# Constants on ScalarE's queue, x in pieces, the last two rows stored by hardware queues, output halves summed on TensorE

## The reference

```
e   = x + par[0]*par[1] * (diag[:, None] * x) @ W     # users: first 2048 rows, items: the rest,
                                                      # each with its own par, diag, W
h   = adj @ (adj.T @ e)
out = layernorm(h) * gamma + beta + x
x   = layernorm(x + out)                              # end of layer 0

T1  = adj @ x;  T2 = 2*adj @ T1 - x;  T3 = 2*adj @ T2 - T1
out = x @ w[0] + T1 @ w[1] + T2 @ w[2] + T3 @ w[3] + bias
x   = layernorm(x + out)                              # end of layer 1, the result
```

## Time and profile before

| | us |
|---|---|
| median of three executions | 1214.84 |
| lowest and highest of them | 1209.78, 1215.15 |
| the profiled execution's own time | 1212.09 |
| its span, first to last instruction | 1210.2 |

### The profile page before, as it was taken

How to read it: one execution, slowest core, us unless ns; L and a number is a source line. 1 busy time by engine, 2 the same in 40 slices (tenths; PEclk the granted TensorE clock), 3 DMA queues, 4 the chain that set the end, 5 groups by cost and what they waited for, 6 DMA issues and landing times.

```text
span 1210.2 us, 13868 instructions
## 1 busy us (share of the span) xinstructions
PE 1109.8 (92%) x5004; PEld 479.3 (40%) x5004; DVE 922.2 (76%) x960; ACT 332.1 (27%) x594; POOL 257.6 (21%) x420
## 2 busy tenths in 40 slices
PE   4999999999999997899889999999999999598794
PEld 3454445444444453444233333344344443122231
DVE  2698798999899898697777766665666667588783
ACT  1456456456466465300000000000100000011010
POOL 0476655464363453100000000000000000011111
PEclk9999999999999999899999999999999999798898
DMA  7999999999999987899999999999999999999991
GB/s 227 300 289 298 282 299 315 289 296 279 299 275 282 296 233 167 186 313 286 266 347 347 336 313 293 318 292 255 261 336 319 336 304 330 348 306 342 353 352 30
DMA packets 372730, 350.82 MB, mean 290 GB/s; under 512 B 11612, under 2 KB 371332, under 8 KB 372692
## 3 DMA queue, kind: packets, MB, share of 16 engines
q1 hardware_dynamic: 259092, 237.35, 70.5%
q10 hardware_dynamic: 110880, 110.11, 31.8%
q0 software_dynamic: 2720, 2.86, 0.9%
HBM read 348.97 MB, written 1.31 MB: 289 GB/s over the span
## 4 chain that ended last, share of the span: by engine, by line
PE 55%; SPq 12%; DVE 12%; ACT 10%; ACTq 5%; issue 4%; POOL 1%; DMA 1%; DVEq 0%; POOLq 0%
PE bank L1174 31%; ACT terms L774 9%; SPq L337 7%; ACTq L279 5%; SPq L326 4%; DVE turned L496 4%; PE bank L1225 4%; PE bank L1187 3%; PE bank L1044 2%; PE bank L1004 2%; PE bank L1032 2%; PE bank L1056 2%; PE bank L1016 2%; DVE shared L516 2%; PE bank L1203 1%
## 5 line engine op out<-in xcount | busy, mean ns | idle before, releaser
L1174 PE MATMUL bank<-turned,terms 128*128 128x512 f32 x680 | 301.4, 596 | 4.5 <-DVE turned L496 3.1
L386 POOL COPY raw<-raw 32x512 f32<-32x512 f32 x320 | 194.8, 609 | 243.6 <-DVE raw L533 205.1
L516 DVE STREAM_TRANSPOSE shared<-shared 32x512 f32<-32x512 f32 x320 | 224.0, 700 | 4.1
L1004 PE MATMUL bank<-shared 128*64 128x256 f32 x1600 | 206.1, 385 | 6.5 <-DMA shared<-in_adj 6.4
L496 DVE STREAM_TRANSPOSE turned<-raw 128x2048 f32<-128x2048 f32 x72 | 165.1, 2301 | 58.9 <-PE bank L1174 50.0
L496 DVE STREAM_TRANSPOSE turned<-shared 128x2048 f32<-128x2048 f32 x68 | 156.0, 2302 | 60.3 <-PE bank L1174 46.0
L774 ACT COPY terms<-terms 32x512 f32<-32x512 f32 x320 | 197.1, 616 | 5.1 <-DVE terms L526 0.9
L1174 PEld LDWEIGHTS bank<-turned,terms 128*128 128x128 f32 x680 | 126.6, 190 | 170.3 <-issue 164.0
L431 POOL DMA_DIRECT2D out<-scratch x40 | 21.7, 549 | 681.1 <-DVE scratch L724 681.0
L1004 PEld LDWEIGHTS bank<-shared 128*64 128x64 f32 x1600 | 111.6, 136 | 88.4 <-issue 33.1
L765 ACT COPY scratch<-bank 128x512 f32<-128x512 f32 x80 | 46.6, 585 | 131.2 <-PE bank L1016 130.9
(11 more groups left out here) (144 smaller groups left out, 1059.7 us busy)
## 6 DMA issues: line engine op xcount, KB each, us to landing
shared<-in_adj SPq DMA_DIRECT2D x100, 1024.0 KB, 10.7
raw<-in_adj SPq DMA_DIRECT2D x106, 512.0 KB, 10.6
raw<-in_adj ACTq DMA_DIRECT2D x106, 512.0 KB, 12.3
shared<-in_adj SPq DMA_DIRECT2D x104, 512.0 KB, 10.6
shared<-in_adj ACTq DMA_DIRECT2D x104, 512.0 KB, 12.1
raw<-in_adj SPq DMA_DIRECT2D x80, 256.0 KB, 7.6
xq<-in_x POOLq DMA_DIRECT2D x40, 32.0 KB, 6.2
out<-scratch POOLq DMA_DIRECT2D x40, 32.0 KB, 5.2
```

Source lines behind the costliest of these rows:

```text
L386: last = nc.gpsimd.tensor_copy(moved[Q32 * c:Q32 * (c + 1), :, :, Q32 * q:Q32 * (q + 1)], beside[Q32 * q:Q32 * (q + 1), :, c, :, :])
L516: last = nc.vector.transpose(low_turned[Q32 * c:Q32 * (c + 1), :, :, Q32 * q:Q32 * (q + 1)], low[Q32 * q:Q32 * (q + 1), :, :, Q32 * c:Q32 ...
L1004: last = nc.tensor.matmul(t_bank[H * odd:H * (odd + 1), 0:PW], e[:, s * SB + b, :], panels[slot][:, s * SB + b, :], start=(k == 0 and b < ...
L1174: last = nc.tensor.matmul(sum_bank[parity][:, :], terms[:, c * GB + i, columns], turned[place][:, i * BANK:(i + 1) * BANK], start=(first a ...
```

## The change

Three parts. First, the head: `W` and `par` are issued by ACT instead of SP; `diag` gets a semaphore of its own, `diag_loaded`, which PE's turning of `diag` now waits for; DVE copies `diag` before it waits for the six other constants; `x` comes by five transfers with a semaphore each, which DVE waits for piece by piece. Second, the end: POOL stores only the first eight rows of the output; SP stores row n = 8 and half of row n = 9, ACT the other half, and SP waits for both rows to land. Third, in `turn_output` each of the four transposes becomes a matmul with `both` as the moving operand, so that the two halves are added in it and 64 columns come out of each; in `finish` the copy and the addition become one copy of 128 x 256.

```diff
         consts_loaded = sem("consts_loaded")
-        x_loaded = sem("x_loaded")
+        diag_loaded = sem("diag_loaded")
+        x_loaded = [sem(f"x_loaded{k}") for k in range(NS)]
...
+        last_stored = sem("last_stored")
...
+        def store(queue, n, q, stored):
+
+            queue.dma_start(quarter(out, ROWS3[n], q),
+                            by_chunk(scratch[Q32 * q:Q32 * (q + 1), 2 + n % 2, 0:GB * H], H)).then_inc(stored, DMA)
+
...
         def _(sp):
-            sp.dma_start(diag_rows[0:UB, :], diag_u.rearrange("(b p) -> b p", p=P)).then_inc(consts_loaded, DMA)
-            sp.dma_start(diag_rows[UB:NB, :], diag_i.rearrange("(b p) -> b p", p=P)).then_inc(consts_loaded, DMA)
-            sp.dma_start(e[:, :, :], x.rearrange("(b p) f -> p b f", p=P)).then_inc(x_loaded, DMA)
-            sp.wait_ge(w_cleared, 1)
-            for k, a in enumerate((W_u, W_i)):
-                for half in range(2):
-                    rows_of = slice(H * half, H * (half + 1))
-                    sp.dma_start(w_pair[rows_of, k, rows_of], a).then_inc(consts_loaded, DMA)
-            for k, a in enumerate((par_u, par_i)):
-                sp.dma_start(par[:, 2 * k:2 * k + 2], a.rearrange("(o n) -> o n", o=1).to_broadcast([P, 2]))\
-                    .then_inc(consts_loaded, DMA)
-
+            sp.dma_start(diag_rows[0:UB, :], diag_u.rearrange("(b p) -> b p", p=P)).then_inc(diag_loaded, DMA)
+            sp.dma_start(diag_rows[UB:NB, :], diag_i.rearrange("(b p) -> b p", p=P)).then_inc(diag_loaded, DMA)
+            x_rows = x.rearrange("(b p) f -> p b f", p=P)
+            for k, s in enumerate(SEGS):
+                b = slice(s * SB, (s + 1) * SB)
+                sp.dma_start(e[:, b, :], x_rows[:, b, :]).then_inc(x_loaded[k], DMA)
...
+            for n in (NG - 2, NG - 1):
+                sp.wait_ge(out_made, n + 1)
+                for q in range(NQ if n == NG - 2 else NQ // 2):
+                    store(sp, n, q, last_stored)
+            sp.wait_ge(last_stored, DMA * NQ * 2)
...
         def _(pool):
-            for n, g in enumerate(ROWS3):
+            for n in range(NG - 2):
                 pool.wait_ge(out_made, n + 1)
                 for q in range(NQ):
-                    pool.dma_start(quarter(out, g, q), by_chunk(scratch[Q32 * q:Q32 * (q + 1), 2 + n % 2, 0:GB * H], H))\
-                        .then_inc(out_stored[n % 2], DMA)
+                    store(pool, n, q, out_stored[n % 2])
             for k in range(2):
-                pool.wait_ge(out_stored[k], DMA * NQ * (NG // 2))
+                pool.wait_ge(out_stored[k], DMA * NQ * (NG // 2 - 1))
...
         def _(dve):
-            dve.wait_ge(consts_loaded, DMA * 8)
+            dve.wait_ge(diag_turned, 1)
+            chain(nc.vector.tensor_copy(diag[:, :], t_bank[:, 0:NB]))
+            dve.wait_ge(consts_loaded, DMA * 6)
...
-            dve.wait_ge(diag_turned, 1)
-            chain(nc.vector.tensor_copy(diag[:, :], t_bank[:, 0:NB]))
-            dve.wait_ge(x_loaded, DMA)
-            for s in SEGS:
+            for k, s in enumerate(SEGS):
                 b = slice(s * SB, (s + 1) * SB)
+                dve.wait_ge(x_loaded[k], DMA)
                 nc.vector.tensor_tensor(xq[:, b, :], e[:, b, :], wide(diag[:, b], SB), ALU.mult).then_inc(x_scaled, 1)
...
-                halves = by_chunk(out_bank[n % 2][:, :], PH)
-                chain(nc.vector.tensor_copy(y, halves[:, :, 0:H]))
-                nc.vector.tensor_tensor(y, halves[:, :, H:PH], y, ALU.add).then_inc(out_taken, 1)
+                nc.vector.tensor_copy(y, by_chunk(out_bank[n % 2][:, 0:GB * H], H)).then_inc(out_taken, 1)
...
         def _(act):
+
+            act.wait_ge(w_cleared, 1)
+            for k, a in enumerate((W_u, W_i)):
+                for half in range(2):
+                    rows_of = slice(H * half, H * (half + 1))
+                    act.dma_start(w_pair[rows_of, k, rows_of], a).then_inc(consts_loaded, DMA)
+            for k, a in enumerate((par_u, par_i)):
+                act.dma_start(par[:, 2 * k:2 * k + 2], a.rearrange("(o n) -> o n", o=1).to_broadcast([P, 2]))\
+                    .then_inc(consts_loaded, DMA)
...
             root(2 * NS + NG - 1, GB)
+            act.wait_ge(out_made, NG)
+            for q in range(NQ // 2, NQ):
+                store(act, NG - 1, q, last_stored)
...
-            pe.wait_ge(consts_loaded, DMA * 8)
+            pe.wait_ge(diag_loaded, DMA * 2)
...
                 for c in range(GB):
-                    last = nc.tensor.transpose(out_bank[i % 2][:, c * P:(c + 1) * P], o_turned[:, c * P:(c + 1) * P],
-                                               ident[:, :])
+                    last = nc.tensor.matmul(out_bank[i % 2][:, c * H:(c + 1) * H], o_turned[:, c * P:(c + 1) * P],
+                                            both[:, :], start=True, stop=True)
```

## The result

| | before | after |
|---|---|---|
| median, us | 1214.63 | 1202.53 |
| lowest and highest of five | 1209.78, 1215.15 | 1199.89, 1205.22 |
| the profiled execution's own time | 1212.09 | 1205.22 |
| its span | 1210.2 | 1203.1 |

The medians differ by 12.1 us. The ratio of the times is 0.9912, with a 95% interval of 0.9886 to 0.9938, which is 10.7 us faster (7.5 to 13.8), against 12.7 predicted.

A forecast was written before the change was run, and what follows sets the result against it. Transfers of `adj` were taken to bound the kernel up to about 170 us, then a cycle of its engines, with 11.36 us without arithmetic at the end. 4.4 + 8.3 + 0 = 12.7 us saved gave 1200 us, range 1194.5 to 1207.

The forecast's parts named there:

- Term 4.4: Head: the first panel of `adj` starts earlier once the constants leave SP's queue; 4.4 us saved, bounds nothing and 5.5.
- the 5.5 of the whole gap: Head: transfer engines nearly idle between `x` and the first panel, 14.7 - 9.2 = 5.5 us, the term's upper bound.
- the 1.1 us taken off for `W`, `par` and the ramp: Head: allowances against the gap, 0.5 us for carrying `W` and `par`, 0.6 for the hand-over to the panel.
- the near end of the two that the prediction kept: Head: constants issued by ACT land near 9 to 10 us, or near 15 if they block behind `x`.
- The sign that failed: Layer 0's first panels: copies of `t` of panels 2, 7 and 20 each some 4.4 us earlier.
- Term 8.3: End: after DVE's last instruction 3.0 us in place of 11.36, POOL's DRAIN lying under sweep 3; 8.3 us saved.
- its upper bound of 9.0: End: with the fastest issues and a landing of 1.8 us, the moved stores save 9.0 us.
- Term 0: Output turning and summing: PE's added work and DVE's saved work cancel in the last row, others are covered; 0 us.
- A: Head: rival, the panel doesn't start earlier, the first term falls to about 0.5 us; 1204 us, chance 0.14.
- B: End: rival, POOL's DRAIN of 7 us stays at the end of the program; 1207 us, chance 0.10.
- C: Head: rival, ACT's constants are starved behind `x` and the panels, landing at 32.6; slower, 1219 us, chance 0.04.

The follow-up runs named there:

- the stores alone: Only the change's stores (rows 8 and 9 by SP and ACT, POOL eight rows) on the kernel before: 1204.71 us, ratio 0.9931.
- the repeat: The whole change once more, same kernel, for a second profile, timed against the kernel before: 1200.48 us, ratio 0.9904.
- the head alone: Only the change's edits of SP, DVE, ACT and PE at the start, on the kernel before: 1209.12 us, ratio 0.9961.
- the cut of the tiles on the kernel before: The kernel before with layer 0's tile loads cut in eight transfers in place of four, nothing else: 1208.77 us, ratio 0.9965.
- turning: Only the summing by the turning matmul, on the kernel before: 1213.3 us, ratio 1.0002.
- row 8 kept: The kernel before with only row 9 stored by SP and ACT, POOL keeping row 8: 1203.94 us, ratio 0.9926.
- `x` in one transfer: The whole change, but x in one transfer as before, in place of five: 1200.38 us, ratio 0.99.

## Why the prediction was right, point by point

**The head.** Term 4.4, measured alone 4.7 (3.3 to 6.3 by the interval). The mechanism is shown by the gap, which goes with the new head and comes back with the constants on SP's queue, and by the lead of the transfers at 8 MB: 4.7 to 5.2 us with the constants on ACT, 0.8 with them on SP. That lead lies between the 4.4 of the term and the 5.5 of the whole gap; of the 1.1 us taken off for `W`, `par` and the ramp, 0.3 to 0.8 are seen. What the prediction did not have is that part of the lead is lost again in the panels behind it. So the gain in time is known less well than the lead: what the whole has beyond the stores alone (0.9912/0.9931, and 0.9904/0.9931 in the repeat) is 2.3 and 3.3 us, each to some 3 us. These and 4.7 agree with 4.4 within their intervals; that the kernel with the head alone came so near to it is in part luck. The waits told rightly that the transfers lead up to about panel 7, as the cut of the tiles on the kernel before shows. The constants issued by ACT were landed at 9.2, by the near end of the two that the prediction kept.

The rule of the Trainium skill that spoke against this term ("DMA: Bandwidth & Descriptors", "Issuing engines are not separate DMA queues") grants a second issuer only its sequencer's time. The traces decide otherwise here: with the six small transfers in SP's queue the engines' share is 0.05 and 0.16 from 10.5 to 13.5 us, with another issuer for them 1.08.

**The sign that failed.** "The copy of `t` of panels 2, 7 and 20 each some 4.4 us earlier" held for the second profile of the same kernel (5.1, 3.8, 3.8) and not for the first (1.7, 0, 0). The prediction had said what it would mean for the copies to be earlier at panel 2 but not at 7: that the engines' cycle led there. That reading is wrong. From panel 2 to 7 a panel takes (170.85 - 55.32)/5 = 23.1 us in the first profile, the engines' cycle is 22.1 by the cut tiles, and the product waits 10.2 us for transfers: they led there too. Two things failed. One is the assumption that one profiled execution gives this number to within a few tenths: for one kernel it moved by 3.9 us at panel 7 (170.85 and 167.00), with times of 1205.22 and 1200.0. The other is that panel 7 moves by as much as the stream starts earlier, some 5 us. In four profiles with the old head (before, stores, turning, row 8 kept) its copy stands at 170.8, 172.5, 171.1 and 170.7, in four with the new one (after, its repeat, the head alone, `x` in one transfer) at 170.9, 167.0, 169.0 and 166.9: 2.8 us earlier in the mean, less than the 4.4 promised. What is left at panel 7 does carry on: from there to panel 20 it is 288.1 to 288.2 us in all of these. Why the transfers of the first panels lose part of the lead, and more of it in the first execution, stays open; the fall of the clock alone does not explain it.

**The end.** Term 8.3, measured alone 8.4 (6.8 to 10.0), and 11.36 - 2.7 = 8.7 in the trace; 3.0 us had been allowed where 2.7 were used. (Two sums of the prediction are a little off here: its pieces of the 11.36 add up to 11.6, since the last landing is counted from an issue that lies inside the 2.30, and its upper bound of 9.0 is 8.7 by the rows that it names, 0.1 + 0.39 + 1.8 + 0.4 left.) SP's last DRAIN took 7 ns where 129 was allowed, and POOL's 6.36 us lie under the last rows. The rule of the Trainium skill on DRAINs ("VectorE: DVE Perf Modes", "The DRAIN you can't avoid"), which made this term 1.3 at most, does not hold for POOL in any profile here: 6.36 to 7.01 us.

**The sum.** Term 0, measured 1.0002. PE's group of the turning is 11.6 us in place of 6.7, as this row of after shows, beside the earlier trace rows:

```profile
L1354 PE MATMUL bank<-both,shared 128*128 128x64 f32 x80 | 11.6, 290 | 0.8 <-ACT shared L949 0.8
```

That is 0.49 more a row, between the 0.4 and 0.6 of the prediction, and DVE's 4.2 less in the window of sweep 3 bought nothing that the time shows. In the last row of the first profile the products took 1.31 us, and the granted clock fell among them, from 1.0 to a mean of 0.67 from 1197 to 1198 us, after TensorE had been busy for 2.54 of the 4 us ahead; in the second profile they took 1.10, and there it cancels: 0.45 more from ACT's end to DVE's copy, 0.46 less on DVE, as in the prediction.

**The total.** 12.7 predicted; 10.7 by the ratio, 11.6 by that of the repeat (9.5 to 13.8), 12.9 by the parts alone. These agree within their intervals, and none of them tells 12.7 from 11.

**The rivals.** A (no earlier panel) is out by the windows, and by the time of the head alone (4.7 us, where A leaves 0.5); its time for the whole, 1204, lies inside the result's interval and would not have told. B (the DRAIN stays) is out: with row 8 kept on POOL it moved with POOL's store. C (constants starved) is out: 9.2 where it needed 32.6.

## What to carry to other kernels

Look at what the first microseconds of a queue wait behind: small scattered transfers that hold the stream of the largest tensor can go to an engine that is idle at that time, as long as the transfer engines are shown idle there. Store the last results by a queue whose DRAIN is short, and leave POOL's DRAIN work to lie beside. Before a mark in the middle of one profile is believed, for or against, see where the profiled execution lies among the others of its kernel, and time the part alone or profile the kernel a second time.

## What the runs showed of the hardware that I had not expected

Loads into 32 partitions in pieces of 512 B ran at 110 to 239 GB/s (repeat of the change, 97 to 104 us) where the panel's segments, into 128 partitions, ran at about 350. The Trainium skill has a rule for the first ("SBUF — State Buffer", "Door 1: The DMA port swizzle"): the rate goes with how many of the 16 ports the partitions reach, and 32 reach half; an estimate from its 435 GB/s is 217. The large transfers stay below that in the mean (185), the cut and mixed ones are somewhat above (235); why they are above is not shown.

Cutting such a load into eight transfers took the kernel before from 22.8 to 22.1 us a panel, and the change from 1200.48 to 1196.91 us.

POOL's DRAIN behind stores of its own queue took 6.36 to 7.01 us in every run, and starts where its last store has landed; those of SP took 7 to 129 ns. POOL's is the same to the nanosecond in all profiles in which POOL stores as many output rows: 7012 ns with ten rows, 6778 with nine, 6359 with eight. No kernel here has POOL store none, so what it would take then is open.
